# Rolling the tile loop of every engine's program into a hardware loop, in a fused block of test-time-training attention, window attention and routed experts

## The chip, the cores and the metric

The kernel runs on one core of one Trainium2 chip. The metric is device time in microseconds (us) of one execution; the time before is the median of three runs. The engines' names are those of the profile: PE is TensorE (PEld its weight loads), DVE VectorE, ACT ScalarE, POOL GpSimd, SP SyncE. A letter q behind an engine's name (PEldq, DVEq) marks an instruction that the engine's sequencer deals with: it reads instructions in order, hands the ones with work to the engine, and keeps waits, register sums and branches for itself.

## What is computed

One transformer block on 2048 tokens of width 256, all in float32, cut here to what matters for the order of the work:

```
xn = layernorm(x)
for each chunk of 128 tokens:                      # a scan: the weights are carried
    out        = fast_mlp(q; W0, W1, W2)           # 4 heads of 64
    dW0..dW2   = gradients from k, v and the learning rates, plus momentum
    dW         = newton_schulz5(dW)                # 5 steps: A = X X^T, B = bA + cAA, X = aX + BX
    W          = renorm(W + dW)
attn = window_attention(xn)                        # 2 heads of 128, window 128
ffn  = shared_mlp(xn) + top-8 of 32 experts(xn)    # 4 groups, the best 2, experts 128 wide
y    = x + (norm(out) * scale + attn) @ Wo + ffn
```

The carried weights make the chunks a chain: chunk i + 1 cannot take its k side before the renormalised W of chunk i is there.

## The kernel before

Each engine has a program of its own, and semaphores between them (their counters only grow). The 2048 tokens are 16 tiles of 128 tokens (`NT` = 16, `LAST` = 15). Every engine's program has a prologue, then `body(0, False)`, then `body(i, False)` for i = 1 to 14, then `body(LAST, True)`. In the kernel before, the loop over 1 to 14 is a Python loop, so the 14 bodies stand one after the other in the instruction stream, and each wait compares a semaphore with a constant.

A body has 20 steps `st` of the Newton-Schulz iteration (`NI` = 5 rounds of four: turn X, Gram matrix, its square, the product with X), each for two groups of two heads (`g` = 0 and 1, tiles `CA0`/`CA1`, `CB0`/`CB1` in PSUM). Between a group's steps stands other work by a table `fill`, written by hand: expert products (`YB`, `HB`, summed on DVE in `acc`), the next tile's projections, window attention, routing.

- One Newton-Schulz round crosses engines: PE `ns_turn` (waits for `X`), ACT `xt` copies `XT`, PE `ns_gram` (waits for `XT`), DVE `ns_a` copies `Am`, PE `ns_pair` (waits for `Am`), DVE `ns_m` makes `Mp`, PE `ns_pair` (waits for `Mp`), DVE `ns_x` makes the new `X` with `aX` from POOL.
- At the end of a body DVE adds `X` to `Wn`, takes row norms (`row_sums`, POOL `row_pow`, `renorm`), PE turns `Wn` (`turn_w`), ACT copies `WT`, and PE starts the next body's `k_side`; ACT copies `ks`, DVE makes `dga` and `dhb`, and PE `grads` follows.
- `routing` on DVE is 13 small steps, each of which waits for the step before it on the semaphore `route_steps`.

The waits of PE on `X`, `XT`, `Am`, `Mp`, `dgba`, `Wn` and `kl_ready`, DVE's on `stats` and `route_steps`, and some of POOL's go through the class `Expect`. It keeps the next value that the semaphore has to reach, waits for it, and raises it by a step. In the kernel before, this value is a Python number:

```
self.eng.wait_ge(self.sem, self.due)
self.due += self.step + skip
```

The other waits have the form `wait_ge(semaphore, a * i + b)` with the tile number `i`.

Of the kernel before, what the change touches and what calls it, by code (L numbers as in the profile page):

```python
# [32 lines left out]
P = 128  # L33
# [28 lines left out]
class Expect:  # L62


    def __init__(self, eng, sem, name, first=1, step=1):
        self.eng, self.sem, self.step, self.due = eng, sem, step, first

    def wait(self, skip=0):

        self.eng.wait_ge(self.sem, self.due)  # L70
        self.due += self.step + skip


def build(nc, x, wall_d, rows_d, wo, fast_d, affine_d, fc1T, fc2T, e1T, e2T, upT, downT, ident_d, fixed_d, out):
    T = x.shape[0]
    NT = T // P
    LAST = NT - 1
    with ExitStack() as ctx:
# [161 lines left out]
        @block.sync  # L240
        def _(sp):
            sp.dma_start(xa[:, :], x[0:P, :]).then_inc(e_xa, 16)
            sp.dma_start(ident[:, :], ident_d[:, :]).then_inc(e_ident, 16)
            for dst, src in ((wall[:, :, :], wall_d[:, :, :]),
                             (rows[:, :], rows_d.partition_broadcast(P))):
                sp.dma_start(dst, src).then_inc(e_const, 16)
            for dst, src in ((fixed[:, :, :], fixed_d[:, :, :]), (affine[:, :, :], affine_d[:, :, :]),
                             (wo_s[:, :, :], wo.rearrange("(k p) n -> p k n", p=P))):
                sp.dma_start(dst, src).then_inc(e_later, 16)

            sp.wait_ge(e_xn, 1)
            sp.dma_start(xa[:, :], x[P:2 * P, :]).then_inc(e_xa, 16)
            sp.dma_start(xr[:, :], x[0:P, :]).then_inc(e_xr, 16)

            def store(i, rows):

                sp.wait_ge(e_ot, i + 1)
                sp.dma_start(out[bass.ds(rows, P), :], ot[:, :]).then_inc(e_stored, 16)

            for i in range(NT - 2):  # L260
                here, after, later = i * P, (i + 1) * P, (i + 2) * P

                sp.wait_ge(e_xn, i + 2)
                sp.dma_start(xa[:, :], x[bass.ds(later, P), :]).then_inc(e_xa, 16)
                store(i, here)

                sp.dma_start(xr[:, :], x[bass.ds(after, P), :]).then_inc(e_xr, 16)
            store(NT - 2, (NT - 2) * P)
            sp.dma_start(xr[:, :], x[LAST * P:T, :]).then_inc(e_xr, 16)
            store(LAST, LAST * P)  # L270
            sp.wait_ge(e_stored, 16 * NT)
# [3 lines left out]
        def _(pool):  # L275
# [73 lines left out]
            def rms_pow(i):  # L349
                pool.wait_ge(e_msq, 2 * i + 2)  # L350
                power(r4[:, 1, :], r4[:, 0, :], neghalf, 4).then_inc(e_rms, 1)
# [5 lines left out]
            def h_sq(i, u):  # L357
                pool.wait_ge(e_hr, NU * i + u + 1)
                if u > 1 or not (isinstance(i, int) and i == 0):
                    pool.wait_ge(e_y, NU * i + u - 1)  # L360
                b = u % 2
                pool.tensor_tensor(hq[b][:, :, :], hr[b][:, :, :], hr[b][:, :, :], ALU.mult).then_inc(e_hq, 1)  # L362

            def body(i, last):
                if last:
                    h_sq(i, 1)
                    h_sq(i, 2)
                    shared_sq(i)
                    h_sq(i, 3)
                    rms_pow(i)  # L370
                    for u in range(4, NU):
                        h_sq(i, u)
                    return
                m = i + 1
                first = i == 0
                k_u(i, 0)
                k_u(i, 1)
                h_sq(i, 1)
                for g in range(G):
                    ss_pow(i, g)  # L380
                prep_rstd(m)
                h_sq(i, 2)
                fill = {0: [lambda: shared_sq(i)], 1: [lambda: h_sq(i, 3)], 3: [lambda: rms_pow(i)],
                        4: [lambda: h_sq(i, 4)], 9: [lambda: prep_n8(m), lambda: h_sq(i, 5)],
                        12: [lambda: h_sq(i, 6)], 14: [lambda: h_sq(i, 7)], 16: [lambda: window(m, first)],
                        17: [lambda: prep_kl(m)]}
                if first:
                    fill[13] = [restore_mask]
                for st in range(4 * NI):
                    if st % 4 == 0:  # L390
                        for g in range(G):
                            ax(i, g, st // 4)
                    for f in fill.get(st, []):
                        f()
                for g in range(G):
                    row_pow(m, g)
                h_sq(m, 0)
# [7 lines left out]
            h_sq(0, 0)  # L405

            body(0, False)
            for i in range(1, LAST):
                body(i, False)
            body(LAST, True)  # L410

# [2 lines left out]
        def _(act):  # L414
# [192 lines left out]
            act.preload_act_table_set("sigmoid_and_others")  # L607
            h_relu(0, 1)
            body(0, False)
            for i in range(1, LAST):  # L610
                body(i, False)
            body(LAST, True)

# [2 lines left out]
        def _(pe):  # L616
# [335 lines left out]
            pe.wait_ge(e_down_w, 16 * NDOWN)  # L952
            pe.wait_ge(e_later, 16 * NLATER)
            body(0, False)
            for i in range(1, LAST):
                body(i, False)
            body(LAST, True)

# [2 lines left out]
        def _(dve):  # L961
# [444 lines left out]
            weights(0)  # L1406
            dve.wait_ge(e_later, 16 * NLATER)
            body(0, False)
            for i in range(1, LAST):
                body(i, False)  # L1410
            body(LAST, True)

# [33 lines left out]
```

## Time and profile before

| | us |
|---|---|
| median of 3 runs (lowest, highest) | 851.59 (851.04, 852.82) |
| the profiled execution: its time | 852.82 |
| its span, from first to last instruction | 850.7 |
| one tile in the middle, e.g. 400.02 to 452.78 | 52.76 |
| PE busy, share of the span | 810.6 (95%) |
| DVE busy, share of the span | 715.0 (84%) |

The profiled execution's time is 2.1 us over its span and 1.2 us over the median. A busy PE here means that a matmul is in its pipeline; it does not mean that it is at its peak. The chain that ended last goes back and forth between PE and DVE, with ACT and POOL in short pieces, and with 6% of "issue": time in which the engine waited for nothing that the profile shows.

### The profile page before, as it was taken

How to read it: one execution, taken by the hardware profiler on the slowest of the kernel's cores; microseconds unless marked ns; L12 is line 12 of the kernel's file. 1: busy time of each engine (PE TensorE's matmuls, PEld its weight loads, DVE VectorE, ACT ScalarE, POOL GpSimd, SP SyncE). 2: the span in 40 equal slices, each digit the busy share in tenths (PEclk: the TensorE clock that was granted, in tenths of full speed). 3: DMA queues.
4: the chain of work that ended last, by engine and by line, in shares of the span. 5: the costliest groups of instructions: out<-in, count | busy, mean ns of one | idle time of the engine just before them, and what ended most of it. 6: DMA issues, size and time to landing. Idle time of an engine off the chain costs nothing.

```text
span 850.7 us, 25189 instructions
## 1 busy us (share of the span) xinstructions
PE 810.6 (95%) x9926; PEld 700.8 (82%) x9926; DVE 715.0 (84%) x2592; ACT 369.2 (43%) x868; POOL 407.1 (48%) x535
## 2 busy tenths in 40 slices
PE   3999999999999999999999999999999999999997
PEld 2888888888888888888888888888888888888886
DVE  4789798897988979889798897988979888798876
ACT  2444344443444444444444444444444453444533
POOL 1644545445454454544554445544465444645442
PEclk9899999999999999999999999999999999999999
DMA  8100000000000000000000000000000000000000
GB/s 320 45 3 14 8 2 21 2 14 8 3 20 3 13 8 3 20 2 15 8 2 20 2 14 8 3 19 3 13 9 2 20 2 14 8 2 14 2 14 7
DMA packets 9813, 15.10 MB, mean 18 GB/s; under 512 B 1121, under 2 KB 8929, under 8 KB 9441
## 3 DMA queue, kind: packets, MB, share of 16 engines
q1 hardware_dynamic: 7904, 7.80, 3.1%
q10 hardware_dynamic: 1792, 5.70, 1.7%
q8 instruction: 79, 1.29, 0.6%
q14 instruction: 38, 0.30, 0.1%
HBM read 11.41 MB, written 2.10 MB: 16 GB/s over the span
## 4 chain that ended last, share of the span: by engine, by line
PE 49%; DVE 36%; issue 6%; ACT 5%; POOL 2%; DMA 1%; SPq 0%; DVEq 0%
PE M L628 13%; PE CB L628 11%; PE HB L628 8%; DVE acc L1320 8%; PE YB L628 6%; PE CA L628 5%; DVE Wn L1167 4%; PE CA L699 4%; DVE Am L1124 3%; DVE Mp L1130 2%; DVE dhb L1087 2%; DVE X L1138 2%; POOL r L284 2%; DVE comb L1245 2%; ACT XT L425 1%
## 5 line engine op out<-in xcount | busy, mean ns | idle before, releaser
L362 POOL TENSOR_TENSOR hq<-hr 128x512 f32<-128x512 f32 x128 | 137.3, 1073 | 77.6 <-ACT hr L425 77.6
L284 POOL TENSOR_TENSOR r<-r,half 128x3 f32<-128x3 f32 (+1 forms) x78 | 78.0, 1013 | 162.0 <-DVE r L1109 67.9
L628 PE MATMUL HB<-xlT,e_s 128*128 128x128 f32 x1024 | 143.4, 284 | 0.4 <-ACT xlT L425 0.4
L628 PE MATMUL YB<-e_s,hq 128*128 128x128 f32 x1024 | 142.5, 282 | 0.8 <-DVE acc L1320 0.8
L425 ACT ACTIVATE hr<-HB 128x512 f32<-128x512 f32 x128 | 76.5, 597 | 131.1 <-PE HB L628 130.9
L1320 DVE SCALAR_TENSOR_TENSOR acc<-YB,cw,acc 128x128 f32<-128x128 f32 x448 | 125.2, 341 | 9.5 <-PE YB L628 9.5
L628 PEld LDWEIGHTS HB<-xlT,e_s 128*128 128x128 f32 x1024 | 127.2, 194 | 6.9 <-ACT xlT L425 0.7
L340 POOL TENSOR_TENSOR aX<-X,a_tile 128x192 f32<-128x192 f32 x150 | 92.9, 640 | 81.5 <-DVE X L1138 81.5
L628 PEld LDWEIGHTS YB<-e_s,hq 128*128 128x128 f32 x1024 | 125.1, 192 | 5.7 <-issue 1.3
L425 ACT ACTIVATE XT<-CA 64x384 f32<-64x384 f32 x150 | 65.7, 477 | 63.7 <-PE CA L699 63.5
L628 PEld LDWEIGHTS CB<-XT 64*64 64x64 f32 x1800 | 59.8, 134 | 21.9 <-ACT XT L425 16.8
L628 PEld LDWEIGHTS CA<-Am 64*64 64x64 f32 x1800 | 60.3, 134 | 20.6 <-issue 11.4
L628 PE MATMUL CA<-Am 64*64 64x64 f32 x1800 | 72.7, 222 | 1.7
L628 PEld LDWEIGHTS CB<-X,Mp 64*64 64x64 f32 x1800 | 58.3, 134 | 17.4 <-issue 8.8
L628 PE MATMUL CB<-XT 64*64 64x64 f32 x1800 | 72.2, 223 | 0.1
L628 PE MATMUL CB<-X,Mp 64*64 64x64 f32 x1800 | 68.6, 222 | 1.4
L1124 DVE COPY Am<-CB 128x192 f32<-128x192 f32 x150 | 50.3, 351 | 22.1 <-PE CB L628 21.0
L1138 DVE SCALAR_TENSOR_TENSOR X<-CB,aX 128x192 f32<-128x192 f32 x150 | 51.0, 349 | 20.2 <-PE CB L628 20.1
L699 PE MATMUL CA<-ident,X 128*64 128x128 f32 x450 | 64.8, 275 | 0.0
L628 PE MATMUL M<-wall,xnT 128*128 128x512 f32 (+1 forms) x128 | 56.9, 551 | 3.5 <-DMA rows<-in_rows 3.5
L1130 DVE SCALAR_TENSOR_TENSOR Mp<-Am,CA 128x192 f32<-128x192 f32 x150 | 48.3, 347 | 5.3 <-PE CA L628 4.8
L699 PEld LDWEIGHTS CA<-ident,X 128*64 128x64 f32 x450 | 45.9, 111 | 4.6
(178 smaller groups left out, 1463.0 us busy)
## 6 DMA issues: line engine op xcount, KB each, us to landing
xa<-in_x SPq DMA_DIRECT2D x16, 128.0 KB, 2.1
e_s<-in_e1T ACTq DMA_DIRECT2D x1, 2048.0 KB, 12.8
e_s<-in_e2T ACTq DMA_DIRECT2D x1, 2048.0 KB, 18.9
xr<-in_x SPq DMA_DIRECT2D x16, 128.0 KB, 2.2
out<-ot SPq DMA_DIRECT2D x16, 128.0 KB, 1.7
wall<-in_wall SPq DMA_DIRECT2D x1, 820.0 KB, 6.1
up_s<-in_upT ACTq DMA_DIRECT2D x1, 512.0 KB, 14.0
down_s<-in_downT ACTq DMA_DIRECT2D x1, 512.0 KB, 20.3
```

The costliest lines, as they stand in the source:

```text
L284: return pool.tensor_tensor(dst, src, expo[:, 0:n], ALU.pow)
L340: pool.tensor_tensor(aX[g][:, :, :].rearrange("p w c -> p (w c)"), X[g][:, :, :].rearrange("p w c -> p (w c)"), a_tile[:, it, :], ALU.mult ...
L362: pool.tensor_tensor(hq[b][:, :, :], hr[b][:, :, :], hr[b][:, :, :], ALU.mult).then_inc(e_hq, 1)
L425: return nc.scalar.activation(out_, in_, func, **kw)
L628: return pe.matmul(out_, lhsT, rhs, start=start, stop=stop)
L699: ins = pe.transpose(CA[g][0:HD, w * P:(w + 1) * P], X[g][:, w, :], ident[:, :])
L1087: tt(dhb[g][:, :], kt[g][:, 0, :], dhi[g], ALU.mult)
L1124: nc.vector.tensor_copy(Am[g][:, :, :].rearrange("p w c -> p (w c)"), CB[g][:, 0:3 * HD]).then_inc(e_am[g], 1)
L1130: nc.vector.scalar_tensor_tensor(Mp[g][:, :, :].rearrange("p w c -> p (w c)"), Am[g][:, :, :].rearrange("p w c -> p (w c)"), b / c, CA[g][ ...
L1138: nc.vector.scalar_tensor_tensor(X[g][:, :, :].rearrange("p w c -> p (w c)"), CB[g][:, 0:3 * HD], NS[it][2], aX[g][:, :, :].rearrange("p w ...
L1167: ins = nc.vector.tensor_scalar(Wn[g][:, w, :], Wn[g][:, w, :], r3[g][:, 5, w:w + 1], nrm[g][:, w:w + 1], ALU.mult, ALU.mult)
L1320: ins = nc.vector.scalar_tensor_tensor(acc[:, e, :], y, w, acc[:, e, :], ALU.mult, ALU.add)
```

## The change

Each engine's Python loop over the middle tiles becomes a hardware loop (`Fori`) over a register. The tile number `i` is then a register, and everything computed from it is too: the 14 bodies are one body in the instruction stream, with a register sum, a compare and a branch at its end. A wait on `a * i + b` compares with a register that an instruction of the sequencer has filled (the rows `ISA`, which multiply, and `REGISTER_ALU`, which add). `Expect` keeps its value in a register in every body, the first one included: the wait stands on the instruction that adds to the register, and the work comes behind it. SP's loop over the loads and stores of the middle tiles is rolled too. POOL's `first` is written so that it still holds for the body with the number 0 alone.

```diff
     def __init__(self, eng, sem, name, first=1, step=1):
-        self.eng, self.sem, self.step, self.due = eng, sem, step, first
+        self.eng, self.sem, self.step = eng, sem, step
+        self.reg = eng.alloc_register(name)
+        eng.reg_mov(self.reg, first)
     def wait(self, skip=0):
-        self.eng.wait_ge(self.sem, self.due)
-        self.due += self.step + skip
+        self.eng.wait_ge(self.sem, self.reg)
+        self.eng.reg_add(self.reg, self.reg, self.step + skip)
...
-            for i in range(NT - 2):
-                here, after, later = i * P, (i + 1) * P, (i + 2) * P
+            with sp.Fori(0, NT - 2) as i:
+                here, after, later = sp.snap(i * P), sp.snap((i + 1) * P), sp.snap((i + 2) * P)
...
-                first = i == 0
+                first = isinstance(i, int)
...
-            for i in range(1, LAST):
+            with pool.Fori(1, LAST) as i:
                 body(i, False)
...
-            for i in range(1, LAST):
+            with act.Fori(1, LAST) as i:
                 body(i, False)
...
-            for i in range(1, LAST):
+            with pe.Fori(1, LAST) as i:
                 body(i, False)
...
-            for i in range(1, LAST):
+            with dve.Fori(1, LAST) as i:
                 body(i, False)
```

Written out engine by engine, the PE program had 1209 rows of different instructions and has 333; DVE's had 1806 and has 402. One PE body now has 351 matmuls, 56 register sums, 3 register products, 23 waits that stand alone and the branch; one DVE body has 249 instructions, 48 of them register sums and 13 register products.

Three places show what moved. The names in brackets are the semaphores that a row waits for, and "x6" means six rows alike.

PE, in the middle of a body, the Newton-Schulz product with `Mp` and the next turn of `X`. Before:

```order
L628 MATMUL CB0<-X0,Mp0 64x64 [waits Mp0]
L628 MATMUL CB0<-X0,Mp0 64x64 x5
L628 MATMUL CB1<-X1,Mp1 64x64 [waits Mp1]
L628 MATMUL CB1<-X1,Mp1 64x64 x5
L780 MATMUL M1<-ident,pr 128x128 [waits qkT_ready,probs]
```

and now:

```order
L73 REGISTER_ALU [waits Mp0]
L630 MATMUL CB0<-X0,Mp0 64x64 x6
L73 REGISTER_ALU [waits Mp1]
L630 MATMUL CB1<-X1,Mp1 64x64 x6
L782 MATMUL M1<-ident,pr 128x128 [waits qkT_ready,probs]
```

The wait has gone from the first matmul of a group to a register sum in front of it; there are 45 such places in a PE body.

DVE, two steps of the routing (`m8`, `mr`) between the two groups' new `X`. Before:

```order
L1138 SCALAR_TENSOR_TENSOR X0<-CB0,aX0 128x192 [waits aX0,product0]
L1284 MAX m8<-msk 128x8 [waits route_steps]
L1138 SCALAR_TENSOR_TENSOR X1<-CB1,aX1 128x192 [waits aX1,product1]
L1287 MATCH_REPLACE mr<-m8,msk 128x32 [waits route_steps]
```

and now:

```order
L1138 REGISTER_ALU
L1139 REGISTER_ALU [waits product0]
L1140 SCALAR_TENSOR_TENSOR X0<-CB0,aX0 128x192 [waits aX0]
L73 REGISTER_ALU [waits route_steps]
L1286 MAX m8<-msk 128x8
L1140 SCALAR_TENSOR_TENSOR X1<-CB1,aX1 128x192 [waits aX1,product1]
```

The wait for PE's product and the wait for the routing step before stand on register sums now, 5 and 13 times in a body.

PE, from the end of one body to the start of the next, before:

```order
L729 MATMUL CA1<-ident,Wn1 64x128 [waits Wn1]
L729 MATMUL CA1<-ident,Wn1 64x128 x2
L628 MATMUL CB0<-WT0,qkT 128x256 [waits WT0,vT_ready,qkT_ready]
L628 MATMUL CB0<-W1BD0,vT 128x128 [waits W1BD0]
```

and now, the end of the loop's body:

```order
L73 REGISTER_ALU [waits Wn1]
L731 MATMUL CA1<-ident,Wn1 64x128 x3
L957 REGISTER_ALU
L957 COMPARE_AND_BRANCH
```

after which the branch leads back to the body's start:

```order
L957 ISA
L630 MATMUL CB0<-WT0,qkT 128x256 [waits WT0,vT_ready,qkT_ready]
L630 MATMUL CB0<-W1BD0,vT 128x128 [waits W1BD0]
```

A sum, a compare with a branch and a product stand between the last turn of `Wn` and the next tile's k side.

## Rows read from the trace of the kernel before

**Rows 1.** The page: busy time, share of the span and instructions of each engine.

```profile
PE 810.6 (95%) x9926; PEld 700.8 (82%) x9926; DVE 715.0 (84%) x2592; ACT 369.2 (43%) x868; POOL 407.1 (48%) x535
```

**Rows 2.** The page: the chain that ended last, share of the span by engine.

```profile
PE 49%; DVE 36%; issue 6%; ACT 5%; POOL 2%; DMA 1%; SPq 0%; DVEq 0%
```

**Rows 3.** Stretches of one tile each: length, busy us (instructions), granted clock, DMA share, GB/s.

```profile
400.02:452.78 52.76, 51.51 (x650) 44.62 (x649) 45.64 (x167) 23.26 (x56) 25.94 (x35) 1.00 0.03 9
452.78:505.60 52.82, 51.56 (x650) 44.68 (x649) 45.70 (x167) 23.32 (x56) 25.99 (x35) 1.00 0.03 9
```

**Rows 4.** The chain in order of time, end of a tile: start us, length us, what.

```profile
434.92 0.04 issue
434.96 0.92 PE CB L628 x24
...
449.29 0.04 issue
449.33 0.53 PE CA L729 x3
449.89 0.32 ACT WT L425
450.22 0.33 ACT WT L425
450.56 0.14 issue
450.69 0.91 PE CB L628 x4
451.62 0.56 ACT ks L425 x2
...
454.31 0.14 issue
454.45 0.70 PE CA L628 x12
```

**Rows 5.** The same chain, where DVE's sequencer and short DVE steps are on it.

```profile
428.17 0.40 issue
428.56 0.02 DVEq L1137
428.59 0.16 issue
...
431.34 0.02 issue
431.37 0.04 DVE t L1267
```

**Rows 6.** Who waited for whom, PEld alone: us in total, times, longest us.

```profile
PEld CA L628 <- issue: 24.3, 30, 1.6
PEld CB L628 <- ACT XT L425: 16.8, 45, 0.8
PEld CB L628 <- issue: 16.6, 59, 0.4
PEld CA L729 <- DVE Wn L1167: 13.0, 30, 1.3
PEld CB L628 <- DVE Mp L1130: 6.8, 30, 0.3
...
PEld CA L628 <- DVE Am L1124: 3.8, 15, 0.3
```

**Rows 7.** The page, a group: busy us, mean ns of one | idle before, releaser.

```profile
L1138 DVE SCALAR_TENSOR_TENSOR X<-CB,aX 128x192 f32<-128x192 f32 x150 | 51.0, 349 | 20.2 <-PE CB L628 20.1
```

**Rows 8.** Line 676 (a wait that stands alone, ahead of the k side): duration ns min/median/max.

```profile
L676 PEldq EVENT_SEMAPHORE  x30: 51/51/51, 26.2 to 767.1; - x30
```

**Rows 9.** The page: DMA queues (packets, MB, share of 16 engines) and an issue's us to landing.

```profile
q8 instruction: 79, 1.29, 0.6%
...
xa<-in_x SPq DMA_DIRECT2D x16, 128.0 KB, 2.1
```

## The prediction

> **What bounds the kernel now.** I read the page first, for the busy shares and for the chain that ended last. PE is busy for 95% of the span and DVE for 84% [rows 1], and the chain is 49% PE and 36% DVE with 6% of issue [rows 2]. So neither engine alone is the bound: work is handed between them all the time, and an added latency at a handover can count in full. Then I cut the middle into tiles. A tile takes 52.76 to 52.82 us, with PE busy 51.5 and DVE 45.6, at a granted clock of 1.00, which is the 2.4 GHz level [rows 3]. The 14 tiles that the change rolls are 14 x 52.8 = 739 us, nearly all of the span. DMA is busy for 3% in them, so transfers bound nothing here. Then I read the chain in order of time at the end of a tile [rows 4]: `Wn` done on DVE, PE turns it, ACT copies `WT`, PE's k side, ACT's `ks`, DVE's steps, PE's gradients. In this stretch every engine waits for the one ahead of it, and nothing covers a delay. It is also where the new branches stand.
>
> **What a wait costs, by where it stands.** This is the measure for the whole sum. Where a matmul itself carries the wait, it starts 0.04 us after the semaphore (434.92 after `Mp`, 449.29 after `Wn`) [rows 4]. Where a wait that the sequencer holds stands in front of it, it is 0.14 us (450.56 after `WT`, 454.31 after `dga`) [rows 4], with the wait itself at 51 ns [rows 8]. On DVE a step that follows its predecessor directly starts 0.02 us after it, while one behind a sequencer's wait needs another 0.02 + 0.16 us, and once a stretch of 0.40 us of issue stands ahead of that wait [rows 5]. The trace of before shows no register sum, no comparison with a register and no branch. For a wait that stands on a register sum I take these as bounds: at least 0.14 - 0.04 = 0.10 us more than now, if the sum goes as fast as a wait that stands alone; at most 0.40 - 0.04 = 0.36 us, if the sequencer reads the next instructions only once the sum is done. I take 0.20, nearer to the low rows because those are on PE itself, but above them because the matmuls behind the sum can't be handed over until it is done, whereas today they lie ready.
>
> **Term 1, PE's waits on register sums.** There are 45 in a body. Most cost nothing: a sum whose semaphore has come while PE still has filler queued is covered. What counts is how many are the last thing that PE waits for. The waits by PEld give that per tile (15 tiles have a body): 45 gaps behind `XT` are 3, 30 behind `Wn` are 2, 30 behind `Mp` are 2, 15 behind `Am` are 1, and the 30 gaps of `CA` put down to issue are 2, which are the gradients behind `dga` [rows 6]. That is 10 per tile. 10 x 0.20 = 2.0 us per tile, in 15 bodies (`Expect` is on registers in body 0 too): **30 us**. With the bounds it is 15 to 54.
>
> **Term 2, DVE's waits on register sums.** A body has 13 on the routing steps and 5 on PE's product ahead of `X0`. Filler hides most: the routing steps stand between Newton-Schulz steps of 0.35 us [rows 7], which run while the sequencer catches up. Exposed are those where the next routing step follows with nothing between (`gs` to `t8` at 431.34, now 0.02 us apart [rows 5], and a few more of that kind), and the one `X` per tile that waits for PE in the open, 20.1 us of idle time before the 150 [rows 7], at one place per tile. I count 5 per tile at 0.16 us, the sequencer's share in [rows 5]: 0.8 us, in 15 bodies **12 us**. It is 0 if all are covered, and 18 x 0.16 x 15 = 43 if none is.
>
> **Term 3, register sums and products without a wait.** They need the sequencer alone, and it runs ahead of the engine. DVE has 249 instructions in a body of 52.8 us where it had about 190 (3048 in 16 bodies). At nothing by cover of the engine's queue; if the cover is gone behind each blocked sum, some ten of 0.05 us [rows 8] are 0.5 us a tile, 7 us in all. ACT's, POOL's and SP's are at nothing for the same reason: ACT is busy 23 of 52.8 us and POOL 26 [rows 3], though in the stretch of [rows 4] ACT's own branch stands between `WT` and `ks`.
>
> **Term 4, the back edge.** It is taken 13 times. PE reaches it when the turn of `Wn1` has been handed over, at about 449.4, and the k side would start at 449.7; so nothing covers it. DVE's and ACT's stand at about the same time and largely overlap PE's. Cheapest is a branch as dear as a standalone wait, 0.10 us or 1.3 us in all. Dearest is a branch whose target has to be read from memory again. The trace shows how the stream comes in: 79 instruction packets of 16 KB on one queue, 0.6% of 16 x 850.7 us, which makes 1.03 us each [rows 9]. They are PE's, since 19,852 matmul and load instructions at 64 bytes are 1.27 MB. A PE body is 1300 of these, 5 of the packets, so its start is 5 packets back when the branch is reached. A fetch that nobody asked for ahead costs its 1.03 us and the way to memory: a 128 KB load needs 2.1 us from issue to landing [rows 9]. So 2.1 us or, as a sum of both, 3.1; if DVE's miss comes behind PE's and not beside it, twice that, 6.2. I take 2.6 us, in the middle of the two: 13 x 2.6 = **34 us**. The bounds are 1 and 81.
>
> The Trainium skill ("Runtime: NRT & Kernel Launch", section "Instruction fetch mechanics") says that instructions are prefetched only sequentially, and that a taken branch out of the current two-page window forces a fetch of the target page before execution goes on. By that rule term 4 stays near its upper half. The same skill ("Advanced Engine Details and Errata", section "Control Flow Timing") gives about 108 ns for a compare and branch; by that figure alone, an estimate, term 4 would be 13 x 0.11 = 1.4 us. No row here decides between them.
>
> **What it removes.** The 79 fetches become fewer or move, and the stream is shorter. They run on queues that are 3% busy, and PE's gaps of issue, 24.3 and 16.6 us [rows 6], are waits at the gradients and behind `XT` at the same place in each tile, not at every 256th instruction. I take 0 for it.
>
> **Sum.** Against the profiled execution of 852.8 us: 30 + 12 + 0 + 34 = 76, so 928.8; the profiled execution is 1.2 us over the median, so 927.6, say **928 us**.
>
> **Rivals.** *The body stays at hand.* If PE's instruction memory holds the 5 or 6 packets of a body, terms 1 and 2 remain and the branch is cheap: 851.6 + 42 + 1 = 895. For it speaks that PE's packets come one at a time and late, so something larger than one packet must lie ready. Chance 0.26, 870 to 905. *Comparisons with a register stop the sequencer too.* The loop's waits that stay on matmuls and DVE steps compare with a register. If the sequencer holds each of those itself, the 0.02 us handovers between dependent DVE steps [rows 5] become 0.18: with some 40 of them on a tile's chain that is 6.4 us, in 14 tiles 90, so 928 + 90 = 1018. Nothing in the trace speaks for or against it. Chance 0.18, 965 to 1070. *Everything is covered.* PE's filler hides the sums, and the branch is cheap: at most 1 us per tile, 851 to 868. Against it is that [rows 4] has no filler. Chance 0.11, of which 0.04 lies within 0.2%. *Faster.* The one mechanism is the instruction stream itself: if PE's issue gaps, 40.9 us in 89 pieces [rows 6], were the sequencer standing at the end of a 16 KB packet, a body that stays at hand would lose up to half, 20 us, so 832 if the waits cost nothing, and it decides from the point where that saving passes terms 1, 2 and 4. Against it is that the gaps recur at the same steps. Chance 0.03. *The change doesn't do what it says:* the written-out program has one body on each engine, so this is left out. My forecast, waits and a refetched body, has 0.42, 900 to 965.
>
> **How the numbers follow.** A measurement of this kernel tells 0.2% (1.7 us) from no change. Faster 0.03, same 0.04, slower 0.93. The range leaves out the covered and the faster case (most of 0.14) and the upper end of the stopped sequencer: 866 to 1015.
>
> **What would show it.** Term 1: the 0.04 us ahead of PE's groups behind `Mp` and `Wn` is 0.14 to 0.40. Term 2: DVE's gaps of 0.02 us between routing steps grow to 0.2, and those between steps that compare with a register stay at 0.02; if these grow too, the stopped sequencer holds. Term 4: in the stretch from `Wn` to the gradients a gap of 2 to 3 us on PE before the k side, and five or more instruction packets per tile as now, against none if the body stays at hand. PE's granted clock stays 1.00; if it fell to the 1.2 GHz level in the new gaps, the time would be beyond the range.

## The result and the profile after

The changed kernel takes **861.7 us** (median of 4 runs, 861.62 to 862.52) against 852.03 for the kernel before beside it: a ratio of 1.0113, 95% interval 1.0099 to 1.0128. So the direction of the forecast was right and its size was not: 9.7 us were lost, not 76, and the time lies below the range of 866 to 1015. It is in the range of the rival *everything is covered*, which had a chance of 0.11.

The page of the changed kernel, the lines that answer to [rows 1, 2, 7, 9] (busy time, instruction queue, chain, the group of the new `X`):

```profile
span 860.0 us, 27595 instructions
...
PE 811.3 (94%) x9926; PEld 700.2 (81%) x9926; DVE 715.6 (83%) x2592; ACT 369.5 (43%) x868; POOL 406.7 (47%) x535
...
q8 instruction: 12, 0.20, 0.1%
...
PE 62%; DVE 26%; issue 7%; ACT 2%; POOL 1%; DMA 1%; DVEq 1%; SPq 0%; ACTq 0%
...
L1140 DVE SCALAR_TENSOR_TENSOR X<-CB,aX 128x192 f32<-128x192 f32 x150 | 49.0, 350 | 22.3 <-PE CB L630 21.0
```

No engine has more work to do: PE and DVE are busy for the same time as in [rows 1] within 0.7 us, so the loss is waiting. The second thing to see is the queue `q8`: 12 packets of instructions where [rows 9] had 79. The stretches of one tile, from one `dhb` to the next, answer to [rows 3]:

```profile
405.33:458.79 53.46, 51.62 (x650) 44.67 (x649) 45.66 (x167) 23.29 (x56) 25.91 (x35) 1.00 0.02 7
458.79:512.20 53.41, 51.57 (x649) 44.59 (x648) 45.61 (x166) 23.24 (x56) 25.87 (x35) 1.00 0.03 8
```

A tile takes 53.4 us instead of 52.8: 0.65 us more, and 15 x 0.65 = 9.75 us is the whole difference. The clock is 1.00 as before. Where in the tile it goes shows in the waits of the weight loads. They can't be set beside [rows 6] cause by cause: nearly all of them are put down to "issue" now and no longer to `XT`, `Am`, `Mp` or `Wn`, since the instruction that waits for those is a register sum, and the matmul behind it waits for nothing that it shows. The idle time of each group of weight loads can be compared; the two that grew most, before and then after (busy us, mean ns of one | idle before):

```profile
L628 PEld LDWEIGHTS CB<-X,Mp 64*64 64x64 f32 x1800 | 58.3, 134 | 17.4 <-issue 8.8 <-DVE Mp L1130 6.8
L699 PEld LDWEIGHTS CA<-ident,X 128*64 128x64 f32 x450 | 45.9, 111 | 4.6
```

```profile
L630 PEld LDWEIGHTS CB<-X,Mp 64*64 64x64 f32 x1800 | 58.8, 135 | 22.1 <-issue 20.3
L701 PEld LDWEIGHTS CA<-ident,X 128*64 128x64 f32 x450 | 46.1, 111 | 7.5 <-issue 2.0
```

The products behind `Mp` wait 4.7 us more and the turn of `X` 2.9 us more, of 9.9 us that PEld idles more in all (its span less its busy time, 159.8 against 149.9). The others change by 1 us or less each: `Am`, `dga`, `WT`, `Wn` and `HB` by 0.5 to 0.8 more, `XT` by 1.0 less. So most of the loss shows behind `Mp` and `X`, which DVE makes.

The chain at the end of a tile, beside [rows 4] (start us, length us, what):

```profile
440.66 0.12 issue
440.78 0.91 PE CB L630 x24
...
455.25 0.12 issue
455.37 0.49 PE CA L731 x3
455.86 0.15 issue
456.00 0.91 PE CB L630 x4
...
460.32 0.12 issue
460.44 0.70 PE CA L630 x12
461.15 0.10 issue
461.25 0.70 PE CA L630 x12
```

Ahead of the products behind `Mp` and of the turn of `Wn` stands 0.12 us now, where 0.04 stood: a wait on a register sum costs 0.08 us more than one on the matmul. Between the turn and the k side, where the branch is, the time from start to start is 0.63 us against 0.36 (449.33 to 449.69 in the trace of before, shown further down). But from the start of the turn to the end of `dga` it is 4.95 us (455.37 to 460.32) against 4.98 (449.33 to 454.31): the branch costs nothing on the chain. And ahead of the first group's gradients stands 0.12 where 0.14 stood: there the kernel before already had a wait of its own in front of the matmul (`kl_ready` and `dgba` both have to come). Ahead of the second group's stands 0.10, where the two groups followed each other without a gap (454.45 and 455.17 in the trace of before).

The same chain on DVE, at two of the steps of [rows 5]:

```profile
434.00 0.03 issue
434.03 0.04 DVEq L1139
434.07 0.12 issue
...
434.22 0.35 DVE X L1140
...
436.24 0.58 DVE gs L1266
436.82 0.03 issue
436.85 0.04 DVEq L73
...
436.93 0.06 DVE t L1269
```

`t` starts 0.11 us after `gs` where it started 0.02 after it, so a routing step that follows directly pays 0.09. From the end of `gs` to the end of the `Mp` behind it, it is 3.84 us (436.82 to 440.66) where it was 3.58 (431.34 to 434.92 in [rows 5] and [rows 4]): 0.26 us of DVE's loss lies in this one stretch, `t` included. Ahead of `X` the gap is 0.22 us.

The sequencers' own instructions (duration ns min/median/max), line 73, the sums of `Expect`, and line 957, the loop of PE:

```profile
L73 PEldq ALU_OP  x673: 32/32/42, 30.2 to 830.2; - x169
L73 DVEq ALU_OP  x210: 40/40/52, 4.8 to 819.7; - x105
...
L957 PEldq COMPARE_BRANCH  x14: 76/207/246, 134.7 to 830.4; - x14
```

A sum takes PE's sequencer 32 ns and DVE's 40. PE's taken branch takes 0.21 us (the last of the 14, which is not taken, 76 ns); no 2 to 3 us stand at any of its turns.

### The profile page after: what moved, and what is told of

It reads as the page before. It is cut to its first block, busy times and chain, and to the rows that moved or that the text cites. A ratio compares the mean times of both kernels' runs of the same rounds, so it can differ in the third digit from the quotient of the medians.

```text
span 860.0 us, 27595 instructions
## 1 busy us (share of the span) xinstructions
PE 811.3 (94%) x9926; PEld 700.2 (81%) x9926; DVE 715.6 (83%) x2592; ACT 369.5 (43%) x868; POOL 406.7 (47%) x535
## 4 chain that ended last, share of the span: by engine, by line
PE 62%; DVE 26%; issue 7%; ACT 2%; POOL 1%; DMA 1%; DVEq 1%; SPq 0%; ACTq 0%
PE CB L630 13%; PE M L630 13%; PE YB L630 11%; PE HB L630 9%; PE CA L630 7%; DVE acc L1322 5%; PE CA L701 5%; DVE Wn L1169 4%; DVE X L1140 2%; DVE dhb L1089 2%; POOL r L286 1%; DVE Am L1126 1%; DVE Mp L1132 1%; DMA rows<-in_rows 1%; DVE r L1233 1%
## 5 line engine op out<-in xcount | busy, mean ns | idle before, releaser
L1140 DVE SCALAR_TENSOR_TENSOR X<-CB,aX 128x192 f32<-128x192 f32 x150 | 49.0, 350 | 22.3 <-PE CB L630 21.0
```

The source lines that it names most:

```text
L1140: nc.vector.scalar_tensor_tensor(X[g][:, :, :].rearrange("p w c -> p (w c)"), CB[g][:, 0:3 * HD], NS[it][2], aX[g][:, :, :].rearrange("p w ...
```

## The experiments

What was open after this: whether the loss is the sums with their waits or the loops, which engine's, how many places count, why the back edge is free, and what it takes for it to be dear. All ratios are against the kernel before on the same chip, with the 95% interval.

The times have a scatter of some us that the middle of the kernel does not have: in the traces, the distance from the first start of `dhb` to the last, which is 14 tiles and 1.85 us, is the same within 0.2 us for kernels that do the same there (740.7, 740.8 and 740.8 us in the first three rows below, whose spans are 850.7, 849.9 and 847.4). Its two ends in the kernel before and in the changed one (duration ns min/median/max, first and last start):

```profile
L1087 DVE TENSOR_TENSOR dhb<-kt,ks x30: 275/700/1124, 30.4 to 771.1; 128x128 f32<-128x128 f32 x30
L1089 DVE TENSOR_TENSOR dhb<-kt,ks x30: 276/702/1125, 31.1 to 781.4; 128x128 f32<-128x128 f32 x30
```

The same for every run, in us:

| kernel | from, to | over before |
|---|---|---|
| before | 30.4, 771.1 | - |
| before, sums that were dropped | 31.2, 772.0 | 0.1 |
| sums ahead of `X` alone | 28.7, 769.5 | 0.1 |
| DVE's `Expect` on registers | 31.4, 773.9 | 1.8 |
| DVE alone rolled | 29.3, 774.4 | 4.4 |
| all but PE rolled | 29.5, 775.5 | 5.3 |
| PE's `Expect` on registers, first time | 29.5, 775.1 | 4.9 |
| the same, second time | 31.0, 776.7 | 5.0 |
| PE alone rolled, first time | 30.2, 775.9 | 5.0 |
| the same, second time | 31.2, 777.0 | 5.1 |
| before with PE's waits alone | 30.2, 777.3 | 6.4 |
| registers without loops | 30.9, 778.2 | 6.6 |
| the changed kernel | 31.1, 781.4 | 9.6 |
| the same, second time | 31.6, 781.8 | 9.5 |
| changed, PE written out | 28.1, 778.4 | 9.6 |
| changed, second wait behind DVE's | 31.4, 782.0 | 9.9 |
| changed with PE's waits alone | 30.4, 782.5 | 11.4 |
| changed, second wait behind PE's | 31.4, 790.8 | 18.7 |
| changed, ten waits at the branch | 28.4, 792.1 | 23.0 |
| changed, two bodies per turn | 27.9, 804.2 | 35.6 |

### Registers without loops, and one engine at a time

Only `Expect` is changed, as in the diff of the change, and the bodies stay written out; SP's loop and the `Fori` of the others are left as before.

```diff
-        self.eng.wait_ge(self.sem, self.due)
-        self.due += self.step + skip
+        self.eng.wait_ge(self.sem, self.reg)
+        self.eng.reg_add(self.reg, self.reg, self.step + skip)
```

> The kernel before with Expect on registers in all 15 bodies, and no loop: the 14 bodies stay written out, all other waits compare with constants, no branch. (Ten or so waits at the end of the PE, DVE and POOL programs keep the registers in use; they are met when they are reached.) The rolled kernel is 9.7 us over before. Theory A, the waits that stand on register sums cost it: this is 8 to 10 us over before, 860 to 862, and a tile takes 53.4 us. Theory B, the back edge and the waits that compare with computed registers cost half or more: 2 to 5 us over before, 854 to 857. PE's start behind a semaphore should be 0.12 us here as in the rolled kernel, against 0.04 before.

861.04 against 852.69: 1.0099 (1.0084 to 1.0113), 8.4 of the 9.7 us. With no loop, no branch and no threshold worked out from `i`, most of it is there. So most of the loss comes with the waits that have moved from the work to a register sum in front of it. The times leave about 1 us for the loops, but the 14 tiles have only 6.6 of the 9.6 us here, which leaves them 3.0; the rest of this run's time lies behind the last `dhb` (81.4 us, where the kernel before has 79.6), where the waits that this run has at the end of each program also stand.

Next, the kernel before with `Expect` on registers and the loop rolled for some engines alone:

```diff
-            for i in range(1, LAST):
+            with pe.Fori(1, LAST) as i:
```

> The rolled kernel with ACT, POOL and DVE written out again on constants; PE (and SP) stay rolled, with PE's 45 waits on register sums a body. Theory A: the cost is PE's, some 9 exposed waits a tile of 0.08 us: 7 to 9 us over before. If DVE's routing waits carry it, this is at most 4 us over before.

> The other half: PE written out on constants, all others rolled. Theory A: 1 to 3 us over before, DVE's sums only, which have filler around them. If DVE's and ACT's waits carry the cost: 6 or more. If this and the run with PE alone rolled add up to the 9.7 us of the rolled kernel, the two costs are independent; if they add up to less, each engine hides part of the other's.

PE alone: 857.04 against 852.69, 1.0053 (1.0040 to 1.0066), +4.4 us. All but PE: 856.48, 1.0047 (1.0035 to 1.0059), +3.8. They add up to 8.1 (in the 14 tiles 5.0 and 5.3, which is 10.3 for 9.6), so the shares are nearly independent, and DVE's side is as heavy as PE's, more than was expected. Then DVE alone:

> DVE's loop rolled with its waits on route_steps and product0 on register sums (and SP's loop, which is idle); PE, ACT and POOL written out with constants. All but PE rolled cost 3.8 us. Theory (a few of DVE's register sums and its branch stand in the open): 3.0 to 3.8 us, 854.5 to 855.5 against 851.5. Rival (the 3.8 us come from ACT's and POOL's programs, whose copies of XT, ks and WT lie between PE's steps): DVE alone at most 1 us, 852.5. If it is in the middle, both have a share.

855.86 against 852.53, 1.0044 (1.0027 to 1.0062): +3.3 by the medians and +3.8 by the ratio. In the 14 tiles it is 4.4 of the 5.3 us of all but PE. So DVE has nearly all of it, and ACT's and POOL's programs together 0.9 us at most. With PE's 5.0 the two make 9.4 of the 9.6 us.

What in DVE's program is it? Two kernels with nothing rolled put only DVE's 14 `Expect` waits (13 of the routing, one of the statistics), or only the wait on PE's product ahead of the first group's `X`, on sums; the second edit:

```diff
-                dve.wait_ge(e_prod[g], 3 * NI * i + 3 * it + 3)
+                if g == 0:
+                    x_in.wait()
+                else:
+                    dve.wait_ge(e_prod[g], 3 * NI * i + 3 * it + 3)
```

> Only DVE's two Expect counters (statistics, routing steps) are kept in registers, nothing is rolled; all else as before. Theory A (the routing steps stand between Newton-Schulz steps and are covered): 0 to 1 us, 851.5 to 852.5. Theory B (they are what DVE loses, each sum taking the place of a wait on the step): 3 to 4 us, 854.5 to 855.5.

> Only DVE's wait on PE's product ahead of the first group's X is moved to a register sum in front of it (5 per tile), nothing is rolled. X stands open behind PE at one place per tile in the profile, and each such place costs 0.1 us more when its wait stands on a sum. Theory (one place in the open): 1.5 us, 853. Rival (all five, or more at each): 4 to 7 us, 855.5 to 858.5. Rival (covered): 0.

The 14 sums cost 1.0020 (1.0010 to 1.0030), 1.7 us, between both theories, and the 14 tiles have 1.8 us too. The sums ahead of `X` cost 1.0004 (0.9991 to 1.0016), and nothing in the tiles. There the kernel before already had a wait of its own in front of `X` [rows 5], and the sum takes its place. Even so, where `X` waits for PE in the open, DVE's idle time grows from 20.1 to 21.2 us, 0.07 at each of 15; it just does not lengthen the tile. The other 2.6 us of DVE's rolled program (4.4 - 1.8) come with its loop: its other sums, the products and the branch. Which of these it is was not told apart. In the trace of the kernel with DVE's `Expect` sums alone `t` starts 0.11 us after `gs` too, as in the changed kernel, and the stretch from the end of `gs` to the end of `Mp` has 3.69 us (433.00 to 436.69), 0.11 more than before; with DVE rolled it has 3.84 (432.26 to 436.10), as in the changed kernel. So one place per tile makes 15 x 0.09 = 1.35 of the 1.7 us, and the loop adds another 0.15 us to the same stretch. That is also why PE's weight loads idle longer behind `Mp` and `X` in the changed kernel: with DVE alone rolled they do so by 4.1 and 2.5 us, while with PE's `Expect` alone on registers (second time) the gain is small everywhere, 1.1 us behind `XT`, 0.7 behind `Am`, `Mp` and `dga`, 0.6 behind `Wn`, 0.3 behind `X`.

A kernel with the sum ahead of the wait, and the wait left on the work, was meant to price the sum by itself:

> The kernel before with one register sum ahead of every Expect wait, into a register that nothing reads; the waits stay on the matmuls and DVE steps with their constants, and nothing is rolled. Theory (what costs is that the wait has gone from the work to an instruction of the sequencer in front of it; a sum without a wait is run ahead of the engine): 0 to 0.5 us, 851.5 to 852. Rival (the sum itself takes the time, 32 ns of the sequencer on PE at some ten places per tile and 40 ns on DVE): 3 to 8 us, 855 to 860.

852.37 against 852.53, 1.0000 (0.9986 to 1.0013). But it tells nothing of sums: nothing reads them, and they were dropped in building (its trace has the 25,189 instructions of before). It was the kernel before, once more. That a sum by itself costs nothing is not shown by it.

### PE's sums alone, and whether PE's loop gives anything back

> Only PE's Expect counters are kept in registers (45 sums with a wait per tile), nothing is rolled. Both on registers cost 8.4 us. If PE's sums are all of PE's loss: 4 to 4.5 us, 855.5 to 856. If DVE's routing sums cost nothing, this one has to carry nearly all of the 8.4: 7 to 8.5 us, 859 to 860, and PE alone rolled would have been cheaper than PE's sums alone.

859.37 against 851.97, 1.0095 (1.0077 to 1.0113), +8.1 us by the ratio and 7.4 by the medians: nearly twice the cost of the same sums in the rolled loop. That called for the rival that the loop gives some time back, by instructions that are not fetched. Three kernels beside each other on one chip test it: the changed kernel with PE's loop alone written out (its counters still in registers), the changed kernel, and PE alone rolled.

```diff
-            with pe.Fori(1, LAST) as i:
+            for i in range(1, LAST):
                 body(i, False)
```

> The changed kernel with PE's 14 bodies written out again, its counters still in registers (the same 45 sums with a wait per tile), all other engines rolled. Theory (a rolled PE loop costs and gives nothing; the difference seen was between chips): within 1 us of the changed kernel on the same chip, 861 to 863. Rival (the loop gives back about 3 us because no instructions are fetched in it): 864 to 866.

> The changed kernel itself on the same chip as the one with PE written out and the one with PE alone rolled: 861 to 862 against 852, as measured first.

> PE alone rolled, on the same chip as the two others. If the difference to PE's sums written out was between chips: 6 to 8 us over before, 858 to 860. If the loop gives 3 us back: 4 to 5 us, 856 to 857, as measured first.

862.63, 862.27 and 856.32 against 852.71: 1.0122, 1.0117 and 1.0044 (1.0027 to 1.0060). With PE written out the page counts `q8 instruction: 82, 1.34, 0.6%`, with PE rolled `q8 instruction: 12, 0.20, 0.1%`, and the time is the same within 0.4 us, the 14 tiles within 0.1. That is the sum of what the fetches cost and what the branch costs, and the chain above has the branch at nothing; so both are nothing that these runs can see. The kernel with PE's sums alone was then run a second time:

> PE's counters alone in registers, nothing rolled, a second time. If the first was the chip's: 3.5 to 5 us over before, as PE alone rolled, 855.5 to 857. If the 8 us are real and only the loop gives part of them back: 7 to 9 us, 859 to 861.

857.42 against 851.86, 1.0059 (1.0045 to 1.0072), +5.0 us. So the 8.1 us did not come back, and it is one and the same kernel: two times on two chips can lie 3 us apart with intervals that do not touch. The traces settle it. In the 14 tiles PE's sums cost 4.9, 5.0, 5.0 and 5.1 us, written out and rolled, in the run with 8.1 us too. What raised the times of that run lies outside these tiles or in executions without a trace.

### How many places count

Where one more wait of the sequencer, long met, stands behind every one of PE's 45 sums, each exposed place grows by what that wait costs.

```diff
         self.eng.reg_add(self.reg, self.reg, self.step + skip)
+        if self.pad:
+            self.eng.wait_ge(Expect.one, 2)
+            self.eng.wait_ge(Expect.two, 16)
```

(Two lines, but one wait more: the second stands on the matmul.)

> The rolled kernel with one more wait, met and standing alone, behind each of PE's 45 waits on sums: each adds some 0.1 us between semaphore and matmul, what ten of them took per piece ahead of the branch (1.05 us for ten). It measures how many of the 45 places are exposed. By PE's share so far, 4.35 us in 15 bodies at 0.08 us a place, 3.6 places: 5.5 us more, 867; with places that become exposed by the longer wait up to 9 more, 871. My prediction's ten places would give 15 or more, 877.

871.89 against 851.32, 1.0239 (1.0224 to 1.0254), 10.2 us over the changed kernel. A wait in a row of them takes 0.105 us (the ten waits further down), so 10.2 / 15 / 0.105 = 6.5 places per tile are in the open, of the 45 on PE, where the prediction had counted ten. With the 0.08 us of a sum that is 6.5 x 0.08 x 15 = 7.8 us if all counted in full from the start; PE alone has 5.0 us in 14 tiles, which is 4.5 places. That some places come into the open only when the wait grows fits this, and was not tested.

The same behind DVE's 14 waits:

> The changed kernel with one or more waits of the sequencer, already met, behind each of DVE's 14 waits of the routing and of the row sums per body. A second wait costs about 0.1 us on PE. Theory (about 3 places per tile of DVE are in the open, each 0.08 us, which make the 3.8 us): with two such waits, 0.2 us, at each, 3 x 0.2 x 15 = 9 us over the changed kernel, 870. Rival (the routing's waits are all covered by the Newton-Schulz steps among which they stand, and what DVE loses it loses at its branch or on ACT): 0 to 2 us over it, 861 to 863. The prediction's five places would give 15, 876.

862.65 against 852.53, 1.0113 (1.0096 to 1.0131): 1.0 us over the changed kernel by the medians, nothing by the ratios, and 0.3 us in the 14 tiles. The expectation counted two waits at each place and there was one, so its 9 us should have been 4 to 5. `gs` to `t` grows by it, from 0.11 us to 0.18:

```profile
436.70 0.56 DVE gs L1271
437.26 0.03 issue
...
437.44 0.06 DVE t L1274
...
440.86 0.27 DVE Mp L1137
```

But from the end of `gs` to the end of `Mp` it is 3.87 us (437.26 to 441.13) against 3.84, so only 0.03 of the 0.07 us get through, and the tile grows by 0.3 / 14 = 0.02. Of the routing's 13 waits one is seen in the open, behind `gs`, where the prediction took five places, four of them in the routing.

### Is it the register, or that the wait has left the matmul?

In the changed kernel, and in the kernel before, PE's `Expect` waits are put on a wait instruction of their own. Its second wait is always met and stands on the matmul; in the kernel before there is no register in it at all.

```diff
+            def alone(sem, due):
...
+                pe.wait_ge(e_init, 2)
+                pe.wait_ge(sem, due)
...
-                ready[g].wait()
+                alone(ready[g], NI * i + it + 1)
```

> The rolled kernel, but PE's 44 waits of the Expect kind that guard Newton-Schulz, gradients and Wn stand alone and compare with a computed register; the sums behind the semaphore are gone (19 sums and 5 fused ones a body, which wait for nothing). Each guarded matmul keeps a wait on a constant that is met. A start behind such a wait should take 0.104 us instead of 0.12 (and 0.04 on constants). If the latency from semaphore to start is all, PE's share of the cost, 4.35 us with PE alone rolled, falls to 0.063/0.079 of it: 861.7 - 0.9 = 860.8. If what costs is that the sequencer is blocked by the sum and hands over the matmuls behind it late, the time falls by 2 us or more.

> The kernel before, no register and no loop, with the same PE waits standing alone on constants ahead of matmuls that wait for a met constant. If the latency of a wait off the matmul is the cause, this alone is 3 to 4 us over before (855.7 to 856.7), nearly as much as PE rolled alone (4.35). If registers or the sums are the cause, it is within 1 us of before.

In the changed kernel: 863.19 against 851.32, 1.0144 (1.0127 to 1.0161), no better than a sum but some 2 us worse (1.8 in the 14 tiles). In the kernel before: 858.30, 1.0085 (1.0070 to 1.0100), +7.0 us without a single register. Its chain, behind `Mp`:

```profile
438.15 0.14 issue
438.29 0.91 PE CB L626 x24
```

0.14 us where the sum leaves 0.12 and the wait on the matmul 0.04. So no register is needed for the loss: it comes when the wait stands on an instruction of the sequencer ahead of the matmul, whichever that is. The prices and the totals agree. 6.4 us in 14 tiles at 0.14 - 0.04 = 0.10 us a place are 4.6 places, and the 5.0 us of the sums at 0.08 are 4.5.

### Why the back edge is free, and when it isn't

Ten waits, long met, are put before PE's branch, in the changed kernel:

```diff
                 body(i, False)
+                for _ in range(10):
+                    pe.wait_ge(e_init, 2)
+                    pe.wait_ge(e_ident, 16)
```

> The rolled kernel with ten satisfied waits that stand alone (51 ns each, 0.51 us) ahead of PE's branch, 14 times. If the back edge is hidden by ACT's copy of WT and DVE's work, and has 0.5 us of cover to spare, the time stays within 1 us of the rolled kernel's 861.7. If PE's way over the back edge is on the chain, all of it counts: 14 x 0.51 = 7.1 us, 869. In between means that the cover is used up in part: from PE's rows (k side 0.63 us after the turn of Wn1, 0.36 before, with the end of dga no later) I expect 2 to 5 us.

874.93 against 852.69, 1.0263 (1.0250 to 1.0276), 13.2 us over the changed kernel, where 2 to 5 were expected. The chain shows what the ten waits took:

```profile
458.81 0.12 issue
458.93 0.49 PE CA L731 x3
459.42 1.19 issue
460.61 0.91 PE CB L630 x4
```

From turn to k side it is 1.68 us instead of 0.63: 1.05 us, or 0.105 for each wait, twice the 51 ns of its record. 14 x 1.05 = 14.7 us were added and 13.2 came out, so 1.5 / 14 = 0.1 us per tile was still hidden at most (in the tiles 13.4 came out, of 13 x 1.05 = 13.65). What covers the branch itself shows in PE's work by time (start us, length us, what, and in brackets the idle time before it). Before:

```profile
449.69 0.60 PE L628 MATMUL CB<-WT,qkT 128*128 128x256 f32 x2
450.12 0.38 PE L628 MATMUL CB<-W1BD,vT 128*128 128x128 f32 x2
450.69 0.67 PE L628 MATMUL CB<-WT,qkT 128*128 128x256 f32 x2 [0.18 <-ACT WT L425]
```

and in the changed kernel:

```profile
456.00 0.67 PE L630 MATMUL CB<-WT,qkT 128*128 128x256 f32 x2
456.51 0.38 PE L630 MATMUL CB<-W1BD,vT 128*128 128x128 f32 x2
456.73 0.64 PE L630 MATMUL CB<-WT,qkT 128*128 128x256 f32 x2
457.20 0.38 PE L630 MATMUL CB<-W1BD,vT 128*128 128x128 f32 x2
```

The k side has two halves. The first needs the first group's `WT`, which has long been there, and the second waits for ACT's copies of the other one. In the kernel before, PE was done with the first half and stood 0.18 us idle until `WT` came. Now the first half starts 0.27 us later behind the turn (0.63 against 0.36), runs right into the second, and the second starts 1.36 us after the turn in both (450.69 - 449.33 and 456.73 - 455.37). The branch moved into a wait that was there anyway, and used it up; that is why ten more waits behind it count nearly in full.

The last kernel doubles the loop's body, so that the branch has to go back 11 packets of instructions and not 5 or 6:

```diff
-            with pe.Fori(1, LAST) as i:
+            with pe.Fori(1, LAST, 2) as i:
                 body(i, False)
+                body(i + 1, False)
```

> The rolled kernel with two bodies in PE's loop, 7 turns instead of 14: some 2850 PE instructions or 11 packets of 16 KB in the loop, where one body has 5.5. The rolled kernel fetched 12 packets in all and none between 131 and 842 us, so its body stays at hand. If 11 packets stay at hand too: no packets in the middle, time as the rolled kernel, 861 to 862. If they don't: some 70 packets again, and 6 taken back edges that find their target gone, of which the prediction's price of 2.1 to 3.1 us less some 0.4 us of cover would make 10 to 16 us: 872 to 878.

887.96 against 851.32, 1.0431 (1.0415 to 1.0446): 26 us over the changed kernel, above both expectations, and this with half the branches. Its page, the branch's durations, and the chain at the first one:

```profile
q8 instruction: 89, 1.46, 0.7%
```

```profile
L957 PEldq COMPARE_BRANCH  x7: 83/3415/3751, 184.9 to 853.2; - x7
```

```profile
184.82 0.49 PE CA L731 x3
185.31 3.36 issue
188.67 2.90 PE CB L630 x8
```

And the stretches around it (columns as in [rows 3]):

```profile
184.50:189.00 4.50, 0.98 (x5) 0.61 (x5) 2.09 (x10) 1.06 (x4) 0.00 (x0) 0.78 0.23 62
189.00:195.00 6.00, 6.00 (x29) 5.52 (x29) 3.63 (x12) 1.49 (x5) 1.96 (x3) 0.59 0.01 3
195.00:205.00 10.00, 9.81 (x131) 9.06 (x131) 7.58 (x25) 4.38 (x10) 6.52 (x8) 1.00 0.06 13
```

Here the mechanism of term 4 is real. The packets are fetched again, each taken branch stops PE for 3.4 us, and while PE stands the granted clock falls: from the 2.4 GHz level at 185.5 to 186.5 us (1.00) to the 1.2 GHz level at 187.5 to 188.6 us (0.50). The mean is 0.78 in the 4.5 us around the gap and 0.59 in the 6 us after it, so most of that stretch runs at the 1.2 GHz level, and in the 10 us after that it is 1.00 again. The eight matmuls of the k side take 2.90 us where they take 1.58 in the changed kernel (456.00 to 457.58), 1.32 us more. Six taken branches at (3.36 - 0.15) + 1.32 would make 27.2 us, and 26.3 were measured, 26.0 of them in the 14 tiles; that is 1.1 to 1.2 us per branch beyond the gap. The rival that a doubled body would halve the branch's cost is out.

## Why the prediction was wrong, point by point

**What bounds the kernel**: right. PE and DVE pass the work to and fro, and small latencies at the handovers are lost time; this is why 0.08 us at a few places makes 1.1%.

**Term 1, PE's sums**: 30 us forecast, 5 measured. The mechanism was right, both sizes were too large. A wait on a sum costs 0.08 us (0.12 - 0.04), below even the lower bound of 0.10, which came from rows with a wait of its own; 0.20 was chosen above all rows without a row for it. And ten places were counted from the number of PEld's idle gaps. A gap is idle time of one engine, not time of the chain: 4.5 places count at the price of a sum. One row was also misread: the 30 gaps of `CA` put down to issue are not two `dga` places a tile. By group of weight loads their 24.3 us are 11.4 ahead of the products with `Am` and 12.9 ahead of the gradients. The first group's gradients could have been left out from the rows: they had 0.14 us in the kernel before, so a sum could add nothing there, and in fact it is 0.12. The second group's had no gap before and has 0.10 now.

**Term 2, DVE's sums**: 12 us forecast; 1.7 to 1.8 measured for the sums of `Expect`, 0 for those ahead of `X`. A direct successor pays 0.09 us, not 0.16, and one place per tile is seen to pay it, not five. The `X` that waits for PE in the open starts 0.07 us later, not 0.16, since a wait of its own stood there already, and the tile is no longer for it. That row was in [rows 5], but was read as a price instead of as a price already paid.

**Term 3, sums without a wait**: 0 on PE, as forecast (written out and rolled alike within 0.4 us). On DVE 2.6 us come with its loop, within the bound of 7 but not the 0 of the sum; the cause is not told apart. With PE's 5.0 and DVE's 1.8 they make 9.4 of the 9.6 us of the 14 tiles.

**Term 4, the back edge**: 34 us forecast, 0 measured on PE. This is the step that failed first of all. The premise was that the branch's target is read from memory again; 12 packets in the whole run, and none from 131 to 842 us, where the kernel before has 68, show that 5 to 6 packets stay at hand. The trace of before could not tell, and the forecast took the refetch as likelier (0.42 + 0.18 against 0.26 + 0.11) on no row. The Trainium skill ("Runtime: NRT & Kernel Launch", section "Instruction fetch mechanics") was cited for it: a taken branch out of the current two-page window forces a fetch. The trace disagrees for this body and agrees for one of 11 packets, where the price of 3.4 us is above even the 2.6 taken. Its 0.11 us for a branch ("Advanced Engine Details and Errata", section "Control Flow Timing") is half of PE's 0.21. The second error stands beside the first: "nothing covers it". PE's wait for ACT's `WT` in the middle of the k side does, for the 0.27 us that the branch adds; it would not have covered 2.6. [rows 4] showed that wait (0.14 of issue at 450.56, behind two `WT` copies), and the prediction read the k side as starting there and at 449.7 both.

**What it removes**: right, 0. PE's packets go from 79 to 12 with no effect on the time.

**The rivals.** *The body stays at hand* had its mechanism right and took over terms 1 and 2 with their sizes, so 895 was wrong as well. *Comparisons stop the sequencer*: its 90 us are out. Waits that stay on the work compare with a register only in the loops, and all that came with the loops is 3.0 us in the 14 tiles. *Everything is covered* named the outcome, at most 1 us per tile (0.65 measured), and in part by luck: its cheap branch was right, but of its covered sums four or five on PE and one on DVE are not. Its counter-argument, that [rows 4] has no filler, overlooked that a step which is ready early is a cover too. *Faster*: out by the kernel with PE written out.

**The chances.** Three sizes, 0.20 us, ten places and 2.6 us, all came out too high, and they were added. For 0.20 no row stood, 2.6 priced a refetch that no row showed, and the rows for the ten counted idle time of one engine. The lower bounds of the terms, 15 + 0 + 0 + 1, give 868; that sum should have had far more weight than 0.11.

## What to carry to other kernels

Price a wait that moves from an instruction to the sequencer in front of it at about 0.08 us per place that is open on the chain, and before counting places, cross out those where the sequencer already stood in front: there it is free. PE's hardware loop cost nothing as long as its body stayed at hand, DVE's cost 2.6 us in 14 tiles beyond its sums; look at the instruction queue's packets, and at the clock behind the branch, before unrolling a loop's body even twice. To count the open places of an engine, put one more met wait behind each and divide; this gave 6.5 where 4.5 counted, so take it as an upper bound. And compare small differences by a stretch of the trace and not by the whole time.

## What the runs showed of the hardware

- A wait in a row of met waits costs PE 0.105 us, though its record says 51 ns; on DVE one more moves the next step by 0.07.
- From semaphore to matmul: 0.04 us with the wait on the matmul, 0.12 on a register sum, 0.14 on a wait of its own. In this kernel 4.5 places per tile count, 5.0 and 6.4 us in 14 tiles.
- PE's compare and branch takes 0.21 us (median 207 ns). DVE's takes 56 ns and ACT's 45.

- A PE loop of 5 to 6 packets is kept, one of 11 is not and stops PE for 3.34 to 3.75 us at each turn; PE's clock then falls for part of the next 6 us, which costs another 1.1 to 1.2 us. A gap of 1.19 us at the same place left the clock at 1.00 in it and in the 9 us behind it.
